# Four layers on one Trainium2 core: the attention layers as one list of 32 samples, the convolution layer begun in the last attention steps and written out, the fourth layer begun in it

## The reference, cut to what matters

```python
x = x + L0(gn(x))   # attention in 8x8 windows: 4 windows a sample, 12 heads of 8, learned bias
x = x + L1(gn(x))   # the same on the image shifted by 4 and 4, 12 heads of 32, masks
x = x + L2(gn(x))   # 3x3 depthwise convolution, then a 96x96 product
x = x + L3(gn(x))   # spikes (clip and round), q k v, k^T v per head, product, 96x96 product
# attention: softmax(q k^T * scale + bias) v, then the output product and its bias
# gn: mean and variance over 3 channels and 256 points of one sample
```

## Time and profile before

| | us |
|---|---|
| median of 3 runs (lowest, highest) | 463.68 (462.47, 466.44) |
| the profiled execution, its own time | 464.35 |
| its span | 462.5 |
| mean granted TensorE clock | 0.973 |

### The profile page before, as it was taken

How to read it: one execution, slowest core, us unless ns; L and a number is a source line. 1 busy time by engine, 2 the same in 40 slices (tenths; PEclk the granted TensorE clock), 3 DMA queues, 4 the chain that set the end, 5 groups by cost and what they waited for, 6 DMA issues and landing times.

```text
span 462.5 us, 13941 instructions
## 1 busy us (share of the span) xinstructions
PE 389.2 (84%) x4971; PEld 283.4 (61%) x4971; DVE 320.8 (69%) x738; ACT 246.5 (53%) x554; POOL 197.8 (43%) x327
## 2 busy tenths in 40 slices
PE   0258689999999887899999999999996989657774
PEld 0258478888888764677777877878774323224331
DVE  0588387787787845767777777777771899545773
ACT  0010457777778555565556666655544534257761
POOL 8102065756766734524444443334452242441231
PEclk9999999999999999999999999999999999768996
DMA  8800000000000000000000000000000000000111
GB/s 281 154 5 1 1 2 4 2 0 0 0 0 0 1 1 1 3 2 3 0 0 0 0 0 0 0 0 0 0 2 2 1 0 0 1 0 17 37 34 52
DMA packets 8511, 7.02 MB, mean 15 GB/s; under 512 B 5058, under 2 KB 8130, under 8 KB 8354
## 3 DMA queue, kind: packets, MB, share of 16 engines
q1 hardware_dynamic: 3984, 5.26, 4.0%
q10 hardware_dynamic: 4498, 1.38, 1.7%
HBM read 5.06 MB, written 1.57 MB: 14 GB/s over the span
## 4 chain that ended last, share of the span: by engine, by line
PE 67%; DVE 17%; issue 5%; ACT 5%; DMA 3%; DVEq 1%; POOL 0%; ACTq 0%
PE bank L748 11%; PE bank L775 11%; PE bank L716 11%; PE bank L757 9%; PE bank L726 6%; DVE conv L1210 5%; PE bank L818 5%; PE bank L1289 3%; PE bank L805 3%; DMA table<-in_L_conv_rpb_table 3%; PE bank L557 2%; PE bank L820 1%; DVE stats L586 1%; DVE row_max L938 1%; ACT kvT L1322 1%
## 5 line engine op out<-in xcount | busy, mean ns | idle before, releaser
L974 POOL TENSOR_TENSOR probs<-probs,row_max 128x384 f32<-128x384 f32 x128 | 105.4, 831 | 124.0 <-DVE row_max L938 123.0
L934 DVE TENSOR_TENSOR probs<-bank,bias 128x384 f32<-128x384 f32 x128 | 65.4, 553 | 56.3 <-PE bank L748 55.7
L839 ACT ACTIVATE probsT<-bank 128x384 f32<-128x384 f32 x128 | 60.9, 492 | 65.7 <-PE bank L757 65.7
L938 DVE TENSOR_REDUCE row_max<-probs 128x6 f32<-128x384 f32 x128 | 68.2, 546 | 0.9
L757 PE MATMUL bank<-cst,probs 128*128 128x128 f32 x384 | 62.3, 280 | 0.0
L748 PE MATMUL bank<-k,q 64*64 64x128 f32 x1536 | 58.0, 282 | 3.9 <-ACT k L884 2.2
L775 PE MATMUL bank<-v,probsT 128*64 128x18 f32 (+1 forms) x1536 | 57.7, 219 | 1.7 <-ACT probsT L839 0.9
L775 PEld LDWEIGHTS bank<-v,probsT 128*64 128x64 f32 x1536 | 50.1, 137 | 13.3 <-issue 11.2
L748 PEld LDWEIGHTS bank<-k,q 64*64 64x64 f32 x1536 | 42.3, 135 | 24.4 <-issue 24.3
L900 DVE COPY v<-bank 64x384 f32<-64x384 f32 (+1 forms) x96 | 46.8, 488 | 11.9 <-PE bank L726 9.7
L716 PE MATMUL bank<-xn,w 128*128 128x256 f32 x192 | 49.6, 382 | 1.4 <-DVE v L900 1.2
(11 more groups left out here) (139 smaller groups left out, 589.7 us busy)
## 6 DMA issues: line engine op xcount, KB each, us to landing
rel_bc<-in_L_conv_rel_index SPq DMA_DIRECT2D x1, 2048.0 KB, 9.9
x<-in_x SPq DMA_DIRECT2D x4, 384.0 KB, 13.1
out_dram<-y_out SPq DMA_DIRECT2D x8, 192.0 KB, 2.1
w<-in_L_conv_w_qkv ACTq DMA_DIRECT2D x1, 432.0 KB, 5.1
cst<-in_consts ACTq DMA_DIRECT2D x1, 421.0 KB
p<-in_L_conv_w_out ACTq DMA_DIRECT2D x1, 144.0 KB, 5.0
pos<-in_L_conv_pos_emb SPq DMA_DIRECT2D x8, 2.0 KB
b_qk<-in_L_conv_qkv_b ACTq DMA_DIRECT2D x8, 0.1 KB, 7.0
```

Source lines behind the costliest of these rows:

```text
L839: nc.scalar.activation(probsT[w][:, :], ps_probsT[w % 2][:, 0:NP * 128], ACT.Exp).then_inc(L.s.probsT_sb, 1)
L934: nc.vector.tensor_tensor(out, scores, b, ALU.add).then_inc(L.s.biased, 1)
L938: nc.vector.tensor_reduce(row_max[w][:, :], probs[w][:, :, :], AX.X, ALU.max).then_inc(L.s.maxed, 1)
L974: nc.gpsimd.tensor_tensor(probs[w][:, :, :], probs[w][:, :, :], by_row(row_max[w]), ALU.subtract).then_inc(L.s.shifted, 1)
```

## The change

- The attention layers are one list: `attention_layers` walks over 32 samples, 16 of L0 and 16 of L1, and gives each body the pairs (layer, sample) of the previous two and the next two, so that at the seam a body has work of both layers. Loops stand only where all five are of the same layer: s = 2 to 11 in L0 and s = 4 to 11 in L1. Everything else is written out, eight steps in a row around the seam (list positions 12 to 19). `first_of` marks sample 0 of L1, where each engine also waits for the last use of what L0 had (banks, scores, divided, turned, y_ready, residual).
- A norm is split in `dve_norm_in` (four steps) and `dve_norm_out` (three, it was four) and is issued inside a body: `norm_in` after the first half of DVE's step, TensorE's small product after the third transpose, `norm_out` at the end of DVE's step, POOL's part (two operations, it was three) at the end of POOL's. TensorE's turn of s-1 waits for `norm_out`, and the second early projection is moved ahead of it. The places: layer 0 half 1 in step 1; layer 1 half 0 in L0's step 12 (it was ahead of step 14); layer 1 half 1 in L1's step 2 (it was behind step 0); layer 2 half 0 in L1's step 12 (it was ahead of step 14).
- L2's pair 0: ACT's pad and first tap at the end of L1's step 14, DVE's taps in step 15, two before and two behind heads(15,0); TensorE's products ahead of out(14) and the pointwise product ahead of out(15). Pair 1: ACT in step 15, DVE behind heads(15,1). The rest of L2 is written out (`pe_l2` and its like), the norm half 1 of layer 2 around pair 2, half 0 of layer 3 around pair 6.
- L3 begins in it: xn of pairs 0 and 1 (ACT) beside pair 7, the spike of pair 0 (DVE) ahead of the statistics of pair 5, the statistics of pair 7 and the norm's half 1 in steps i = -1 and 0.

The core of the diff:

```diff
-            step(nc.vector.tensor_scalar(gn_mean[:, of], ps_mix[0:C, 0:HB], float(SPAN), None, ALU.mult))
-            step(nc.vector.tensor_scalar(gn_negmean[:, of], gn_mean[:, of], -1.0, None, ALU.mult))
-            step(nc.vector.tensor_tensor(gn_m2[:, :], gn_mean[:, of], gn_mean[:, of], ALU.mult))
-            step(nc.vector.tensor_tensor(gn_var[:, :], ps_mix[0:C, HB:2 * HB], gn_m2[:, :], ALU.subtract))
+            step(nc.vector.tensor_scalar(gn_negmean[:, of], ps_mix[0:C, 0:HB], -float(SPAN), None, ALU.mult))
+            step(nc.vector.tensor_tensor(gn_m2[:, :], gn_negmean[:, of], gn_negmean[:, of], ALU.mult))
+            step(nc.vector.scalar_tensor_tensor(gn_veps[:, :], ps_mix[0:C, HB:2 * HB], EPS, gn_m2[:, :], ALU.add, ALU.subtract))
...
+        def pe_sample(pe, cur, prev, prev2, nxt, nxt2, norm):
...
             pe_transpose(pe, L, s, 2)
+            if norm:
+                pe_mix_norm(pe, *norm, prev2 or (L, -1))
             if nxt2:
-                pe_qkv(pe, L, moved(s, 2), 0, 1)
+                pe_qkv(pe, *nxt2, 0, 1)
             pe_transpose(pe, L, s, 3)
+            if norm:
+                pe_qkv(pe, *nxt2, 1, 2)
+                pe.wait_ge(gn_step, gn_count(*norm) * STEPS)
             if prev:
-                pe_turn(pe, L, moved(s, -1), 1)
-            if nxt2:
-                pe_qkv(pe, L, moved(s, 2), 1, 2)
+                pe_turn(pe, *prev, 1)
+            if nxt2 and not norm:
+                pe_qkv(pe, *nxt2, 1, 2)
...
+            one(0)
+            one(1, (0, 1))
+            loop(L0, 2, B - 4)
+            one(B - 4, (1, 0))
+            for i in range(B - 3, B + 2):
+                one(i)
+            one(B + 2, (1, 1))
+            one(B + 3)
+            loop(L1, 4, B - 4)
+            one(2 * B - 4, (2, 0))
+            for i in range(2 * B - 3, 2 * B):
+                one(i)
...
+        def pe_last(pe):
+            pe_values(pe, L1, B - 1, 1)
+            pe_turn(pe, L1, B - 1, 0)
+            pe_taps(pe, 0, 0)
+            pe_out(pe, L1, B - 2)
+            pe_turn(pe, L1, B - 1, 1)
+            pe_pointwise(pe, 0, 0)
+            pe_out(pe, L1, B - 1)
...
+        def dve_l2(dve):
+            dve_norm_in(dve, 2, 1)
+            for j in range(2, PAIRS):
+                dve_depthwise(dve, j, j % 2)
+                if j == 2:
+                    dve_norm_out(dve, 2, 1)
+                if j == 6:
+                    dve_norm_out(dve, 3, 0)
+                if j == 7:
+                    dve_l3_spike(dve, 0, 0)
+                dve_l2_stats(dve, j - 2)
+                if j == 5:
+                    dve_norm_in(dve, 3, 0)
+            dve_l2_stats(dve, PAIRS - 2)
```

More of the change, by code:

```diff
@@ L766, in pe_values @@
                 wait(pe, L.s.divided, pair_count(s, j - 1))
+                if first_of(L, s) and j == 0:
+                    pe.wait_ge(L0.s.divided, B)
             elif j == 0:
@@ L799, in pe_turn @@
             wait(pe, L.s.heads_sb, heads_before(L, s, j, 1))
+            if first_of(L, s) and j == 0:
+                pe.wait_ge(L0.s.heads_sb, B)
             if j == 1:
                 wait(pe, L.s.y_ready, s * 1)
-            pe_mix_normed(pe, L, s, B - 3)
+                if first_of(L, s):
+                    pe.wait_ge(L0.s.y_ready, B)
             rows = 128 if L.wide else C
@@ L821, in pe_out, with pe_mix_norm @@
             last.then_inc(L.s.out_ready, 1)
+        def pe_mix_norm(pe, layer, half, read):
+            L, s = read
+            wait(pe, L.s.y_ready, s + 1)
+            pe_group_norm(pe, layer, half)
         def act_norm(act, L, s):
-            act.wait_ge(gn_done, 2 * gn_count(L.n, 0))
+            gn_ready(act, L.n, 0 if isinstance(s, int) and s < HB else 1)
             if isinstance(s, int) and s < 2 and L.n:
@@ L938, in dve_max, with dve_scores @@
             nc.vector.tensor_reduce(row_max[w][:, :], probs[w][:, :, :], AX.X, ALU.max).then_inc(L.s.maxed, 1)
-        def dve_scores(dve, L, s, j, between=None, heads=None):
+        def dve_scores(dve, L, s, j, between=(), heads=()):
             for u in range(NU):
@@ L944, in dve_scores @@
             dve_max(dve, L, s, 2 * j)
-            if heads is not None:
-                dve_heads(dve, L, heads, 1)
+            if heads:
+                dve_heads(dve, *heads, 1)
             elif between:
-                evacuate(dve, "dve", L, *between)
+                evacuate(dve, "dve", *between)
             dve_max(dve, L, s, 2 * j + 1)
@@ L1145, in pool_first, with attention_layers, sample_of, one @@
-        def pool_first(pool, L, before):
-            if before:
-                pool_residual(pool, before, B - 2)
+                    pool_shift(pool, *nxt, w)
+            if norm:
+                pool_group_norm(pool, *norm)
+        def attention_layers(eng, body):
+            def sample_of(i):
+                if i < 0:
+                    return None
+                return (L0, i) if i < B else (L1, i - B) if i < 2 * B else None
+            def one(i, norm=None):
+                body(eng, *(sample_of(i + d) for d in (0, -1, -2, 1, 2)), norm)
+            def loop(L, first, end):
+                with eng.Fori(0, (end - first) // 2) as i:
+                    for par in range(2):
+                        at = Sample(i + first // 2, par)
+                        body(eng, *((L, moved(at, d)) for d in (0, -1, -2, 1, 2)), None)
+            one(0)
[10 more added lines that the diff above has]
+                one(i)
@@ L1148, in pool_first, with act_first, dve_first @@
+        def act_first(act):
+            for s in range(2):
+                act_norm(act, L0, s)
+                for i in range(2):
+                    evacuate(act, "act", L0, s, i)
+        def dve_first(dve):
+            evacuate(dve, "dve", L0, 0, 2)
+            dve_scores(dve, L0, 0, 0)
+        def pool_first(pool):
             for w in (0, 1):
-                pool_shift(pool, L, 0, w)
-            if before:
-                pool_residual(pool, before, B - 1)
+                pool_shift(pool, L0, 0, w)
@@ L1465, in _ @@
[L1465 to L1473 removed]
+            dve_first(dve)
+            attention_layers(dve, dve_sample)
+            dve_last(dve)
```

455 lines of the change are left out of this document (205 added, 250 removed).

## The result

The changed kernel takes 443.24 us (median of 4 runs, 442.12 to 444.06), the kernel before on the same chip 464.9 us (462.47 to 466.44): a ratio of 0.954, 95% interval 0.948 to 0.959. The span of its profiled execution is 441.4 us against 462.5, its mean granted clock 0.987 against 0.973. The forecast was 443.5, with 439 to 452 as its range.

A forecast was written before the change was run, and what follows sets the result against it. Steady attention steps are bound by TensorE, so only three transition gaps could shrink: 7.4 (seam) + 0 (other norms) + 8.05 (convolution) + 5.0 (fourth layer) = 20.5 us off 464.35, forecast 443.5, range 439 to 452.

The forecast's parts named there:

- Part 1, steps 13 to 17: Seam from L0 to L1: mixed steps sum to 43.25 us plus 1.95 of waits, replacing 54.99; gain 7.4, bounds 4 and 9.3.
- The two norms at the seam: Norms moved out of the old seam stretch cost 1.5 us in L0 and 0.9 in L1, together bounded by 1.0 and 3.5.
- The other norms keep about their price: Norms away from the seam, moved inside steps and one DVE and one POOL operation shorter: gain 0, bounds -1 and +1.
- Part 2: L2's pairs 0 and 1 begun in L1's last steps: 8.05 us gained by L3's first product, bounds 5.5 and 9.
- Part 3, pair 0 to pair 1: L3's first link takes 4.3 us instead of 7.97 at full clock: 3.7 gained, 2.2 with a low clock.
- Part 3, pairs 1 to 4: L3's next pairs lose the low clock but take in stats(7) and a norm, 2.1 us: 1.3 gained, bounds 0 and 2.3.
- From pair 4 on nothing changes: L3 from pair 4 to the end: no gain or loss.
- 1 (the seam drains): TensorE waits behind ACT work of both layers at the seam, part 1 gives 3 instead of 7.4 us: 448; 12%.
- 3 (code loading): Written-out attention steps and convolution wait for instruction blocks; at 1.5 us a block it costs 30: 474; 3%.
- 4: A misread order undoes the overlap and only the fourth layer's ramp gains: 459; 4%.
- rival 2: Second half gives part back: pair 2 begins 2 us later, low clock at L3's start, part 3 gives 2: 448.5; 15%.

The follow-up runs named there:

- seam_bubble: Changed kernel with the next sample's third q/k product ahead of the first transpose on PE, in step 15 alone, ACT's order unchanged: 444.16 us, ratio 0.9577.
- best: Changed kernel with the edit of spike2_first, plus the third q/k product and its ACT evacuation moved ahead in steps 15, 16 and 17: 440.99 us, ratio 0.9493.
- norm_old: Changed kernel with the norm in its old form, eight DVE steps and three POOL operations, at the new places: 447.46 us, ratio 0.9634.
- seam_drained: Changed kernel with the seam between L0 and L1 drained again, everything behind it as changed: 450.22 us, ratio 0.9685.
- unrolled: Changed kernel with both hardware loops of the attention layers written out, all 32 steps as straight code: 443.3 us, ratio 0.9544.
- spike2_first: Changed kernel with DVE's spike of pair 2 ahead of pair 7's statistics and norm (3,1)'s input, PE's norm product one step later: 440.53 us, ratio 0.9484.
- l3_late: Changed kernel with L3's first normalised pair and first spike behind all L2 statistics again, norm (3,1) ahead of pair 1: 448.83 us, ratio 0.9658.
- best_warm: Kernel of best with 15 unread matmuls in four PE waits at the end of L3: 439.57 us, ratio 0.9455.
- l2_late: Changed kernel with L2's pairs 0 and 1 begun only behind L1's last output, on all engines: 449.42 us, ratio 0.9651.

## Why the prediction was right, and where it was not

- **Part 1, steps 13 to 17.** Forecast 43.25 + 1.95 = 45.20, measured 45.67. Step by step, with the waits: 6.87 (6.87), 7.74 (7.73), 10.20 (10.05), 10.21 (9.96), 10.65 (10.59). Swapping pieces of the steady chains held to 0.25 us a step, and the three waits of 0.65 are there, and for the reason given: with the third qk alone moved, the wait of step 15 grew to 1.02 (seam_bubble), and with ACT's evacuation moved too the waits shrank to 0.32 or went (best). The part gains 54.99 - 45.67 - 1.43 - 0.91 = 7.0 against a forecast of 7.4. Undone, the seam costs 6.0: the drained seam is 0.4 shorter than the old one, and 0.6 of the 7.0 belong to the form and place of the two norms. The bounds 4 and 9.3 were not the sum's own: its lowest terms together give 54.99 - 43.25 - 3.5 - 1.95 - 3.2 = 3.1, its highest 10.7.
- **The two norms at the seam.** 1.5 and 0.9 forecast, 8.30 - 6.87 = 1.43 and 11.71 - 10.80 = 0.91 measured.
- **"The other norms keep about their price ... 0, bounds -1 and +1."** The total held, the working did not. In the attention layers the two norms meant here gain 0.7: L0's steps 0 and 1 take 14.21 us instead of 14.62, L1's steps 12 and 13 take 22.51 instead of 22.84. But the shorter form, priced at about nothing, is worth 1.9 us over the four norms of L0 and L1 and 3.4 in the whole trace (norm_old), 1.6 of it because in L0 the dropped DVE step and its neighbour ran beside POOL at 0.37 and 0.75 us instead of 0.17 and 0.16. That it came out near nothing is luck: L0's new place costs 0.5 of it. The prediction had read the same effect in the earlier trace rows and used it for one norm, not for the form. And the 1.7 us of the norm's second part behind the taps sat unnamed in part 2's sum.
- **Part 2.** The last y_attn ends 17.49 us after L1's last scores instead of 14.90: 2.6 later, forecast 3.2. Pair 2 begins 6.8 earlier, forecast 6.2; pair 2 to pair 7 takes 25.10 us, forecast 25.4. L3's first product, counted from L1's last scores, comes 50.28 us behind instead of 59.31: 9.0 gained, forecast 8.05, at the upper bound of 9: 0.6 more at pair 2, 0.3 between pair 2 and pair 7, 0.1 behind it. The mechanism and the order of the waits were right; the sizes were all on the careful side.
- **Part 3, pair 0 to pair 1.** 3.89 us, forecast 4.3, at the full clock as forecast. The nine products were priced too high, 2.6 us where they took 2.11.
- **Part 3, pairs 1 to 4: "about half of them hidden: 1.3 gained".** Measured 0.3 (19.20 against 19.51). This step failed, in the clock more than in the overlap. The prediction let the stop ahead of the first product go and with it the low clock for good, and put 1.05 us on pair 7's statistics and the norm. But these stood ahead of DVE's spike of pair 2, PE waited 2.81 us, and the clock fell again behind that wait. With PE kept busy in it the link takes 18.38, 1.2 above the 17.2 of later pairs, about the 1.05 allowed; the 0.8 between 18.38 and 19.20 is the clock, which the sum had at nothing. With the spike first (17.28) even the allowed cost goes.
- **"From pair 4 on nothing changes."** The code doesn't, but it took 34.45 us instead of 34.02; without a change of code it took 33.2 to 34.6 in these runs.
- **Sum.** 20.5 forecast, 464.9 - 443.2 = 21.7 measured, 21.1 by the spans. These are 0.4 in the preparation, 7.0 at the seam (7.4 forecast), 0.7 for the other norms (0), 9.0 up to L3's first product (8.05) and 4.0 in L3 (5.0). Errors of up to 1 us cancel, so the closeness of 443.2 to 443.5 is partly luck.
- **Rivals.** 1 (the seam drains) and 3 (code loading) are refuted by seam_drained and unrolled, 4 by every undone part. Of rival 2 only a low clock came, later than it said and for 0.8 us. The parts undone one by one sum to 7.0 + 6.2 + 5.6 + 4.2 = 23.0 by the medians, 1.3 more than the whole change, and from the first scores of the traces to 6.0 + 5.7 + 4.7 + 3.4 = 19.8, 0.9 less than the whole (20.7). Neither difference is clear of what runs and clock vary by. What the granted clock does from one execution to the next (0.987 to 0.994 in spike2_first, 1 to 2 us of its span) is not explained by any run here.

## What to carry to other kernels

When engines work through fixed lists, price a merged transition by swapping pieces of the steady chains, and then look for what a moved instruction stands ahead of: here a block of DVE work in front of the one short instruction that TensorE needed cost 1.1 us by itself and 0.8 by the low clock behind it. A short vector step that read only SBUF and met a GpSimd operation in L0 lasted until that operation ended, two to five times its length alone, so look first there for steps to drop or fuse, if TensorE waits for them; where GpSimd was idle the same step cost 0.2. Before the end of a stage of small matmuls is tuned further, see what its granted clock is in several executions, and try filling the waits.

## What the runs showed of the hardware

In L3 a low clock came behind waits of PE: behind 3.12 us of standing still the nine first products took 4.08 and 3.52 us (kernel before, l3_late), without it 2.11; behind 2.81 us three products came to take 1.48, and with nine unread matmuls in that wait they stayed at 0.81. But the same code at L3's begin ran at 1.00 in one profiled execution (best, 387 to 399) and at 0.72 in another (best_warm, 388 to 400); what sets it there no run shows. All attention steps as straight code (40 instruction packets instead of 25) cost nothing that can be measured.

DVE's SBUF-only norm steps took 0.15 to 0.18 us alone. Where one began beside a POOL operation of 0.8 us or more, it ended within 0.03 us of that operation's end: those of 0.37 and 0.75 above, one of 0.83 in L1's norms (198.24 against 198.21), one of 1.24 in l2_late (358.63 against 358.60). In the other direction POOL's residual took 2.00 us instead of 1.14 beside DVE's taps. The Trainium skill, "SBUF — State Buffer", section "Who interferes with whom", says that a VectorE instruction with two SBUF inputs and a GpSimd instruction that reads SBUF contend, and that the order of issue decides which is blocked; the trace agrees in both directions. The step of 0.37 us reads one SBUF tile only and waited too, which that rule does not cover.
